# Second pass of the first stage: router sums as a 129th column of the transposes, the third norm's variance from the second's, tokens written in place

## The reference, cut to what matters

```python
h = _L0_tok_ref(x, L0_tok_W)                                 # (16, 512, 128)
h = h + _L0_attn_ref(_layernorm(h, axis=-1), W1, W2)         # softmax(scores) @ x
h = h + _L0_ffn_ref(_layernorm(h, axis=-1), ...)             # second norm: x

# inside _L0_ffn_ref
pooled = x.mean(axis=1)                                      # over the 512 tokens
h = gelu(pooled @ router_w1.T + router_b1)
route = softmax(h @ router_w2.T + router_b2)
idx_s, idx_t = argmax(route[:, :K]), argmax(route[:, K:])
xn = _ln(x, norm_s_w, norm_s_b)                              # third norm, the same
xt = _ln(x, norm_t_w, norm_t_b)                              # with other weights
```

## Time and profile before

| | us |
|---|---|
| median of 3 runs (lowest to highest) | 1715.43 (1713.93 to 1717.41) |
| the profiled execution | 1713.09 |
| its span | 1711.3 |
| PE busy in it | 1534.3 (90%) |
| DVE busy | 1244.6 (73%) |
| ACT busy | 1102.3 (64%) |
| POOL busy | 1019.1 (60%) |

### The profile page before, as it was taken

One profiled execution on the slowest core, in us unless ns is written; L12 is line 12 of the kernel. 1 busy time (PEld: TensorE's weight loads), 2 busy tenths in 40 slices (PEclk: granted clock), 3 DMA queues, 4 the chain that ended last, 5 costly groups with the idle time before them and its releaser, 6 DMA issues. The chain is left out here.

```text
span 1711.3 us, 37358 instructions
## 1 busy us (share of the span) xinstructions
PE 1534.3 (90%) x8662; PEld 661.7 (39%) x8662; DVE 1244.6 (73%) x3454; ACT 1102.3 (64%) x2137; POOL 1019.1 (60%) x1375
## 2 busy tenths in 40 slices
PE   3758967899999999999999999999999999875998
PEld 1216953233333333333333333333333333212765
DVE  6886867488787887878787787878788787453442
ACT  3324850747877778787877778787777878824333
POOL 7832434567576667658567666757667775422443
PEclk9868975979999999999999999999999999957999
DMA  1221117365356456446446545546545644030221
GB/s 50 75 51 33 44 44 98 45 84 77 61 80 75 69 67 84 62 65 82 66 69 76 80 60 78 76 58 80 75 70 67 84 56 61 2 38 27 62 67 56
DMA packets 134645, 109.27 MB, mean 64 GB/s; under 512 B 24128, under 2 KB 127552, under 8 KB 134592
## 3 DMA queue, kind: packets, MB, share of 16 engines
q1 hardware_dynamic: 132544, 104.45, 41.3%
q0 software_dynamic: 2048, 4.20, 1.0%
HBM read 19.26 MB, written 8.39 MB: 16 GB/s over the span
## 5 line engine op out<-in xcount | busy, mean ns | idle before, releaser
L1122 ACT ACTIVATE probs<-psum 128x512 f32<-128x512 f32 (+3 forms) x1536 | 749.5, 549 | 276.0 <-PE psum L1230 269.7
L1022 DVE TENSOR_REDUCE mx_S<-psum 128x1 f32<-128x512 f32 x512 | 324.7, 679 | 58.5 <-PE psum L1210 58.3
L1022 DVE TENSOR_REDUCE mx_C<-psum 128x1 f32<-128x512 f32 x512 | 317.6, 676 | 35.6 <-PE psum L1210 35.6
L1018 DVE CUSTOM_DVE_ANT_0 psum<-psum,causal 128x128 f32<-128x128 f32 (+3 forms) x512 | 241.3, 515 | 102.0 <-PE psum L1210 101.0
L1210 PE MATMUL psum<-ks_S,qs_S 96*128 96x512 bf16 x512 | 198.0, 398 | 17.2 <-DVE mx_S L1022 8.1
L1210 PE MATMUL psum<-ks_C,qs_C 96*128 96x512 bf16 x512 | 200.0, 398 | 12.0 <-DVE mx_C L1022 9.5
L1230 PE MATMUL psum<-qs_S,ks_S 99*128 99x512 bf16 x512 | 189.6, 386 | 5.4 <-ACT probs L1122 5.4
L1230 PE MATMUL psum<-qs_C,ks_C 99*128 99x512 bf16 x512 | 189.0, 387 | 4.7 <-ACT probs L1122 4.3
L903 POOL CAST parts_q<-f_q 128x512 bf16<-128x512 f32 x48 | 29.2, 609 | 255.8 <-ACT f_q L1113 255.4
L1210 PE MATMUL psum<-ks_T,qs_T 96*128 96x128 bf16 (+3 forms) x512 | 158.0, 311 | 4.8 <-DVE mx_T L1018 3.4
L1230 PE MATMUL psum<-qs_T,ks_T 99*128 99x256 bf16 (+3 forms) x512 | 152.1, 301 | 6.9 <-ACT probs L1122 4.2
(11 more groups left out here) (182 smaller groups left out, 2724.6 us busy)
## 6 DMA issues: line engine op xcount, KB each, us to landing
qs_S<-parts_q SPq DMA_DIRECT2D x96, 128.0 KB, 4.4
ks_S<-parts_k SPq DMA_DIRECT2D x96, 128.0 KB, 4.9
qs_T<-parts_q SPq DMA_DIRECT2D x96, 128.0 KB, 4.5
ks_T<-parts_k SPq DMA_DIRECT2D x96, 128.0 KB, 4.6
...
```

The lines of the kernel that those rows point to most:

```text
L1018: nc.vector.tensor_tensor_reduce(tile[:, 0:last_key], tile[:, 0:last_key], causal[:, T - last_key:T], 1.0, NEG, ALU.add, ALU.max, mx[kind] ...
L1022: nc.vector.tensor_reduce(mx[kind][:, n:n + 1], tile, AX_X, ALU.max, negate=True).then_inc(reduced, 1)
L1122: nc.scalar.activation(probs[:, group_place(kind, b, n // 4), n % 4, t0:T], psum[:, LOGITS + ring_place(kind, b, n, RC), t0:T], ACT.Exp, s ...
```

## The change

Five things are done differently in the second pass.

- The normalised tokens are written by DVE into X in place, not into `xs`, so ACT's copy to X goes, and its semaphore `x_stored`.
- The third norm takes its variance from the second: var3 = var2 * rstd2 * rstd2, in two POOL multiplications, plus eps and the power; its mean is taken to be zero. DVE's second set of statistics and `shift3` go. ACT's `again` is then a Copy with a scale and reads X.
- The pooling products go. POOL writes sqrt(var3 + eps), as (var3 + eps) * rstd3, beside the identity, as column 128 of `turner`, and `turn` multiplies `xh` by these 129 columns. So column 128 of each product is the sum of the 128 tokens before the third norm. The transposes thereby become true float32 products, in banks 6 and 7, two tiles to a bank.
- ACT copies the four sum columns to `pooled4` behind the copy to xhatT. DVE adds them up once at the end, and the 1/512 is the scale of the router's GELU.
- `turner` also holds the `xs` of the first pass (rows of 129 columns); POOL copies eight identities into it between the passes, and PE waits for that before its first logits.

```diff
--- before.py
+++ after.py
@@ -183,7 +183,7 @@
         rw2 = sb("rw2", [P, 2 * K])
         rb2 = sb("rb2", [B, 2 * K])
         place = sb("place", [B, K])
-        mean_col = sb("mean_col", [P, 1])
+        pooled4 = sb("pooled4", [P, B, NB])
         h = sb("h", [P, B * NB, P])
         six = sb("six", [P, NB, 6])
         mv = sb("mv", [P, NB, 2])
@@ -191,12 +191,13 @@
         rstd = sb("rstd", [P, NB])
         mv2 = sb("mv2", [P, 2, NB, 2])
         rstd2_t = sb("rstd2_t", [P, 2, NB])
-        mv3 = sb("mv3_t", [P, NB, 2])
-        rstd3_t = sb("rstd3_1", [P, NB])
-        shift3 = sb("shift3", [P, NB])
+        rstd3_t = sb("rstd3_1", [P, 2, NB])
         vare2 = sb("vare2", [P, NB])
+        once3 = sb("once3", [P, NB])
+        var3_t = sb("var3_t", [P, NB])
         vare3 = sb("vare3_t", [P, NB])
-        xs = sb("xs", [P, 2, NB, P])
+        turner = sb("turner", [P, 2, NB, P + 1])
+        xs = turner[:, :, :, 0:P]
         xh = sb("xh", [P, NB, P])
         xT = sb("xT", [P, T])
         parts = sb("parts", [64, NPART, B, T], BF16)
@@ -243,16 +244,15 @@
         h2_saved = sem("h2_saved")
         six2, stats2, var2, rstd2 = sem("six2"), sem("stats2"), sem("var2"), sem("rstd2")
         x_ready = sem("x_ready")
-        x_stored = sem("x_stored")
-        six3, stats3, var3, rstd3 = sem("six3"), sem("stats3"), sem("var3"), sem("rstd3")
-        shift_ready = sem("shift_ready")
+        scaled3, var3, eps3, rstd3 = sem("scaled3"), sem("var3"), sem("eps3"), sem("rstd3")
+        turner_made, weighted = sem("turner_made"), sem("weighted")
         xh_ready = sem("xh_ready")
         turned2 = sem("turned2")
         xhatT_kept = sem("xhatT_kept")
-        pooled_in = sem("pooled_in")
         r_pe, r_act, r_dve = sem("r_pe"), sem("r_act"), sem("r_dve")
         expert_in = sem("expert_in")
-        MAXIMA, LR, TURN, POOLED = 4, 5, 6, 7
+        MAXIMA, LR, TURN = 4, 5, 6
+        turned = psum[:, TURN:TURN + 2, :].rearrange("p a (c e) -> p a c e", c=2)
         LOADS = 7
         HALF_AT = B
         LO_LAG, SCORE_LAG, MAX_LAG = 4, 6, 7
@@ -300,7 +300,6 @@
             @block.gpsimd
             def _(pool):
                 nc.gpsimd.memset(ident[:], 0.0)
-                nc.gpsimd.memset(mean_col[:], 1.0 / T)
                 nc.gpsimd.memset(eps_t[:], EPS)
                 nc.gpsimd.memset(minus_half[:], -0.5)
                 nc.gpsimd.iota(place[:], pattern=[[1, K]], base=-K, channel_multiplier=0,
@@ -330,21 +329,45 @@
                     if exists(b - LO_LAG):
                         low_part(b - LO_LAG)
 
-                def root(stats, var, done, number, mv, vare, rstd, used=None):
-
-                    pool.wait_ge(stats, number + 1)
-                    at_least(pool, done, number)
-                    nc.gpsimd.tensor_tensor(vare[:], mv[:, :, 1], eps_t[:], ALU.add).then_inc(var, 1)
-                    pool.wait_ge(var, number + 1)
-                    if used:
-                        at_least(pool, used, number)
-                    nc.gpsimd.tensor_tensor(rstd, vare[:], minus_half[:], ALU.pow).then_inc(done, 1)
+                pool.wait_ge(x_kept, B)
+                pool.wait_ge(turned1, B)
+                nc.gpsimd.tensor_copy(turner[:, :, :, 0:P].rearrange("p a n e -> p (a n) e"),
+                                      ident[:].unsqueeze(1).broadcast_to([P, 2 * NB, P])).then_inc(turner_made, 1)
+
+                def second_root(b, odd):
+
+                    pool.wait_ge(stats2, b + 1)
+                    nc.gpsimd.tensor_tensor(vare2[:], mv2[:, odd, :, 1], eps_t[:], ALU.add).then_inc(var2, 1)
+                    pool.wait_ge(var2, b + 1)
+                    nc.gpsimd.tensor_tensor(rstd2_t[:, odd, :], vare2[:], minus_half[:], ALU.pow).then_inc(rstd2, 1)
+
+                def third_root(b, odd):
+
+                    pool.wait_ge(rstd2, b + 1)
+                    nc.gpsimd.tensor_tensor(once3[:], mv2[:, odd, :, 1], rstd2_t[:, odd, :], ALU.mult).then_inc(scaled3, 1)
+                    pool.wait_ge(scaled3, b + 1)
+                    nc.gpsimd.tensor_tensor(var3_t[:], once3[:], rstd2_t[:, odd, :], ALU.mult).then_inc(var3, 1)
+                    pool.wait_ge(var3, b + 1)
+                    at_least(pool, weighted, b)
+                    nc.gpsimd.tensor_tensor(vare3[:], var3_t[:], eps_t[:], ALU.add).then_inc(eps3, 1)
+                    pool.wait_ge(eps3, b + 1)
+                    at_least(pool, xh_ready, b - 1)
+                    nc.gpsimd.tensor_tensor(rstd3_t[:, odd, :], vare3[:], minus_half[:], ALU.pow).then_inc(rstd3, 1)
+
+                def weigh_tokens(b, odd):
+
+                    pool.wait_ge(rstd3, b + 1)
+                    at_least(pool, turned2, b - 1)
+                    nc.gpsimd.tensor_tensor(turner[:, odd, :, P], vare3[:], rstd3_t[:, odd, :], ALU.mult)\
+                        .then_inc(weighted, 1)
 
                 def roots(b, odd):
                     if exists(b):
-                        root(stats2, var2, rstd2, b, mv2[:, odd, :, :], vare2, rstd2_t[:, odd, :])
+                        second_root(b, odd)
                     if exists(b - 1):
-                        root(stats3, var3, rstd3, b - 1, mv3[:], vare3, rstd3_t[:], xh_ready)
+                        weigh_tokens(b - 1, 1 - odd)
+                    if exists(b):
+                        third_root(b, odd)
 
                 halves_of_pairs(pool, roots, 1, B // 2, B // 2 + 1)
 
@@ -436,29 +459,19 @@
                                 in1=tokens(h, b, n), op0=ALU.mult, op1=ALU.add)
                         last.then_inc(h2_ready, 1)
                         dve.wait_ge(h2_ready, b + 1)
+                        at_least(dve, scaled3, b - 1)
                         settle(nc, scrap)
                         statistics(lambda n: tokens(h, b, n), b, six2, stats2, mv2[:, odd, :, :])
-                    if exists(b - 2):
-                        dve.wait_ge(rstd3, b - 1)
-                        at_least(dve, xh_ready, b - 2)
-                        nc.vector.scalar_tensor_tensor(out=shift3[:], in0=mv3[:, :, 0], scalar=-1.0, in1=rstd3_t[:],
-                                                       op0=ALU.mult, op1=ALU.mult).then_inc(shift_ready, 1)
                     if exists(b - 1):
-                        at_least(dve, xh_ready, b - 2)
                         dve.wait_ge(rstd2, b)
-                        at_least(dve, pooled_in, b - 2)
-                        at_least(dve, x_stored, b - 2)
-                        normalise(lambda n: xs[:, 1 - odd, n, :], lambda n: tokens(h, b - 1, n),
+                        normalise(lambda n: tokens(X, b - 1, n), lambda n: tokens(h, b - 1, n),
                                   mv2[:, 1 - odd, :, :], rstd2_t[:, 1 - odd, :], x_ready)
-                        dve.wait_ge(x_ready, b)
-                        settle(nc, scrap)
-                        statistics(lambda n: xs[:, 1 - odd, n, :], b - 1, six3, stats3, mv3)
 
                 halves_of_pairs(dve, second_norms, 2, B // 2, B // 2 + 1)
 
 
-                dve.wait_ge(pooled_in, B)
-                nc.vector.tensor_copy(pooled[:], psum[:, POOLED, 0:B]).then_inc(r_dve, 1)
+                dve.wait_ge(xhatT_kept, B)
+                nc.vector.tensor_reduce(pooled[:], pooled4[:], AX_X, ALU.add).then_inc(r_dve, 1)
                 dve.wait_ge(r_pe, 2)
                 nc.vector.tensor_tensor(rl[:], psum[0:B, 1, 0:2 * K], rb2[:], ALU.add).then_inc(r_dve, 1)
                 dve.wait_ge(r_dve, 2)
@@ -514,20 +527,20 @@
                     nc.scalar.activation(probs[:, odd, :, :], psum[:, 0:4, :], ACT.Exp, scale=SCALE_D).then_inc(exped, 1)
 
                 def keep(b, odd):
+                    act.wait_ge(turned2, b + 1)
+                    nc.scalar.activation(xhatT[:, bass.ds(b, 1), :].rearrange("p o (a c e) -> p (o a) c e", a=2, c=2),
+                                         turned[:, :, :, 0:P], ACT.Copy)
+                    nc.scalar.activation(pooled4[:, bass.ds(b, 1), :].rearrange("p o (a c) -> p (o a) c", a=2),
+                                         turned[:, :, :, P], ACT.Copy).then_inc(xhatT_kept, 1)
+
+                def again(b, odd):
+
                     act.wait_ge(x_ready, b + 1)
-                    act.wait_ge(summed, b + 1)
-                    nc.scalar.activation(X[:, bass.ds(NB * b, NB), 0:P], xs[:, odd, :, :], ACT.Copy).then_inc(x_stored, 1)
-                    act.wait_ge(turned2, b + 1)
-                    nc.scalar.activation(xhatT[:, bass.ds(b, 1), :].rearrange("p o t -> p (o t)"),
-                                         psum[:, TURN, :], ACT.Copy).then_inc(xhatT_kept, 1)
-
-                def again(b, odd):
-
-                    act.wait_ge(shift_ready, b + 1)
+                    act.wait_ge(rstd3, b + 1)
                     at_least(act, turned2, b)
                     for n in range(NB):
-                        last = nc.scalar.activation(xh[:, n, :], xs[:, odd, n, :], ACT.Identity,
```

(15 more changed lines are left out.)

## The result

| | median us (lowest to highest) | runs |
|---|---|---|
| kernel before | 1715.93 (1713.93 to 1717.41) | 4 |
| changed kernel | 1728.26 (1727.62 to 1731.19) | 4 |

The ratio is 1.0076, with a 95% interval of 1.0059 to 1.0093. Forecast was 1715.0 us, with a range of 1711.2 to 1717.8; the changed kernel is 12 us slower. The profiled execution of the changed kernel took 1731.19 us with a span of 1728.4, 17.1 us more than that of before.

What follows compares the result with a forecast made beforehand. PE's own work was taken to bound the second-pass loop, the loop through h 0.26 us behind and binding after the change. Loop -1.8 and tail +1.4 gave -0.4 us: 1715.0 us against 1715.43, range 1711.2 to 1717.8.

Steps and rivals of the forecast that it cites:

- a shift in the second stage: Leftover case outside the changed first stage, for what no row shows; no size given, chance 0.03.
- The loop: Second pass, batches 3 to 15: the chain mix, reciprocal, h, mix binds; twelve distances total 66.6 us, gain 1.8 us.
- PE's address step: Instruction carrying PE's wait for h ahead of the mix, batches 6 to 13: 0.13 us each, bounds nothing to double.
- PE's own 5.36 us: PE's work per second-pass batch after the change: mix 3.68, turn 0.92, logits 0.76 us; 0.36 less than before.
- The tail: Last turns behind batch 15's reciprocal, paced by ACT and PE: copies end at 15.6 us, 1.4 us later than before.
- normalisation: ACT's four scaled copies per batch, on the path in the tail's turn cycle: 1.65 us.
- Costs taken as nothing: ACT's small copy (0.27 us), POOL's longer chain (about 3.5 us) and the identity copy: hidden, no cost in time.
- The copy of the identity: POOL's one-time copy into turner between passes: 1.2 to 2.3 us, stalling DVE but hidden behind PE's stacking wait.
- The fast clock in the tail: Rival: PE at 2.4 GHz in the last three turns saves 2.3 us, giving 1712.7 us; chance 0.12.
- No gain in the loop: Rival: address step and hand-overs eat the 0.36 us, distances stay 5.70 us, giving 1716.8 us; chance 0.08.
- DVE held by POOL: Rival: POOL's busier chain delays h's multiply-adds on the shared path, 0.35 us per batch, giving 1719 us; chance 0.04.
- more passes: Rival: the identity product takes four times the transposes, 1.88 us per batch, giving 1728 us; chance 0.03.

Runs made afterwards that it cites:

- before_dve60: Kernel before with 60 one-element VectorE memsets between the first stage's passes, loop start 936, 40 modulo 128 as in the changed kernel: 1732.19 us, ratio 1.0082.
- after_dve36: Changed kernel with 36 one-element VectorE memsets in the second pass's head, second-stage loop start 844: 1714.09 us, ratio 0.9980 against the kernel before.
- the five slow programs: The changed kernel, it with 16 VectorE memsets, and the kernel before with 34, 44 or 60: 52 to 55 instruction loads each, 1728.26 to 1789.51 us.
- after_dve68: Changed kernel with 68 one-element VectorE memsets, second-stage loop start back at 876 as in the kernel before: 1714.42 us, ratio 0.9981 against the kernel before.
- a36_pe_out: Changed kernel with 36 VectorE memsets and PE's second pass written out without a loop: 1711.79 us, ratio 0.9974 against the kernel before.
- a_both_out: Changed kernel with PE's and VectorE's second passes both written out and 118 VectorE memsets: 1709.94 us, ratio 0.9964 against the kernel before.
- a36_identity: Changed kernel with 36 VectorE memsets and ScalarE's four scaled copies as Identity with zero bias instead of Copy: 1714.55 us, ratio 0.9990 against the kernel before.

## Why the prediction was wrong, point by point

**The step that failed: the second stage had no term.** The text said that "the rest of the span matters only if it is moved", and asked only whether it is moved in time. It was moved in the instruction store. Into the sum went each engine's time in the second pass, and nothing for how many instructions each engine has ahead of the loops behind it. The case stood among the rivals as "0.03 for what no row shows, a shift in the second stage", without place or price. Its size is +14 us (before_dve60 against before, by the ratio; 15 by the medians) to +16 us (the changed kernel against after_dve36), four times all else together. What could have been seen before: nothing in the trace of before gives the position or the price, since no load falls into the second stage there. But the two programs could be counted (68 instructions less ahead of VectorE's longest loop), and this should have been a case with a mechanism and a wide price, on the slower side.

On fetching, the Trainium skill ("Runtime: NRT & Kernel Launch", section "Instruction fetch mechanics") gives most engines 32 KiB of instruction memory, and says that a taken branch to a target outside of the current pages has to fetch it first. The 32 KiB agree with these runs: three blocks of 8 KiB of a body and one ahead fit, four and one don't. So does the branch: in the five slow programs VectorE waits 2.5 to 4.2 us behind the jump back. The refill in blocks of 16 KiB that it states is not what VectorE's queue shows here (0.45 MB in 55 loads), and the period of the experiments, 128 instructions, is half of such a block.

**The loop: right.** Forecast were distances of 5.36, three of 5.47 and eight of 5.60, together 66.6 us and a gain of 1.8; in after_dve36 and after_dve68 they are 66.57 us and 1.84. The changed kernel's own profile has 66.84, since one distance (170.53 to 176.26) was 5.73. The 0.13 for PE's address step, taken from the like step on VectorE, is confirmed by a36_pe_out: 1.13 us less, 0.14 in each of the eight. That PE's own 5.36 us would be the next floor was too high by at least 0.26 us (a_both_out).

**The tail: wrong sign.** Forecast was the last copy to `xhatT` and `pooled` at 15.6 us behind the reciprocal of batch 15, 1.4 us later than before (14.27). The tail of the changed kernel, which answers to the earlier trace rows:

```profile
234.79 1.76 PE L627 MATMUL psum<-turner,xh 128*128 128x129 f32 x8 [1.90 <-ACT xh L542]
...
240.57 0.60 ACT L531 ACTIVATE xhatT<-psum 128x512 f32<-128x512 f32 x1 [2.18 <-PE psum L627]
241.07 0.17 ACT L533 ACTIVATE pooled<-psum 128x4 f32<-128x4 f32 x1
241.12 1.27 ACT L542 ACTIVATE xh<-X,rstd 128x128 f32<-128x128 f32 x4
...
242.44 2.09 PE L627 MATMUL psum<-turner,xh 128*128 128x129 f32 x8 [1.90 <-ACT xh L542]
244.57 0.60 ACT L531 ACTIVATE xhatT<-psum 128x512 f32<-128x512 f32 x1 [2.18 <-PE psum L627]
245.06 0.17 ACT L533 ACTIVATE pooled<-psum 128x4 f32<-128x4 f32 x1
...
246.54 0.27 ACT L557 ACTIVATE rh<-psum,rb 128x16 f32<-128x16 f32 x1
```

The copies end at 245.23, 13.20 us behind 232.03, and GELU follows 1.31 us later as before. The mechanism was right: the turns are paced by ACT and PE in turn. The second turn ends 4.5 us behind the reciprocal (forecast 5.5), and the cycle from there on is 4.00 us (240.57 to 244.57) and not 4.61. Its terms: turn 2.09 (forecast 1.96), normalisation 1.27 (forecast 1.65), and the two copies 0.55 until the normalisation begins (forecast 0.89, from a GELU of 0.27; the copy of four columns takes 0.17 and begins before the large one has ended). So the tail is 1.07 us shorter in the changed kernel (17.89 from reciprocal to expert transfer, 18.96 before), and 1.66 us shorter in after_dve36 (17.30), where the first turn still has the full clock. a36_identity puts back the normalisation's mis-sized duration alone and gives 19.24, longer than before: this term, with the clock of the first turn that hangs on it, decided the sign.

**Costs taken as nothing: right.** ACT and POOL cover their added work in the loop (the distances are those of h alone). The copy of the identity took 1.03 us on POOL (from 117.23), under my lower bound of 1.2. It did hold DVE, as forecast for its full length: two small operations beside POOL's (a cast and the `ng_r` behind it) took 3.04 us from start to end, and 2.05 in before_dve60, which has no such copy. As forecast too, it cost nothing: PE waits 4.41 us for a stacking transfer behind it.

**The rivals.** The fast clock in the tail came in part, for one of three turns (1.76 us in the changed kernel, 1.16 in after_dve36); the last two are at half clock. "No gain in the loop", "DVE held by POOL" and "more passes" did not happen. The last of them named 1728 us, and so does the result, but that is chance: the eight passes take 0.97 us of loads, not 1.88, and PE waits in the loop.

**The sum put right**: -1.8 (loop), -1.1 to -1.7 (tail), and +14 to +16 for the loads in the second stage, against +12.3 between the two medians. Without the loads the change is worth -3.5 us by the traces, and 0.9980 and 0.9981 by the runs.
